# Attention's PSUM banks: two pairs for scores, one for row maxima, joins head by head through the shared bank

## The reference

```python
scores = jnp.einsum('bhid,bhjd->bhij', q, k) * scale     # 2048 x 2048 for each head
scores = jnp.where(causal_mask, scores, min)             # first layer only
attn = jax.nn.softmax(scores, axis=-1)
out = jnp.einsum('bhij,bhjd->bhid', attn, v)
out = out.transpose(0, 2, 1, 3).reshape(b, n, HEADS * HEAD_DIM) @ w_out
```

## Time and profile before

| | us |
|---|---|
| runs shown: median (lowest, highest) | 5976.87 (5966.03, 5989.33) |
| the profiled execution | 5959.15 |
| its span | 5957.9 |
| first attention, steps | from 110 to 1195 |
| second attention, steps | from 2320 to 2957 |
| third attention, steps | from 3280 to 4150 |
| fourth attention, steps | from 4436 to 5889 |

### The profile page before, as it was taken

How to read it: one execution, slowest core, us unless ns; L and a number is a source line. 1 busy time by engine, 2 the same in 40 slices (tenths; PEclk the granted TensorE clock), 3 DMA queues, 4 the chain that set the end, 5 groups by cost and what they waited for, 6 DMA issues and landing times. The chain is left out here.

```text
span 5957.9 us, 69438 instructions
## 1 busy us (share of the span) xinstructions
PE 4932.2 (83%) x27568; PEld 2398.2 (40%) x27568; DVE 3519.1 (59%) x5322; ACT 2358.2 (40%) x3274; POOL 1865.1 (31%) x900
## 2 busy tenths in 40 slices
PE   6888898957767776777767999998679999999996
PEld 3444444445445553333333222222344444444443
DVE  4667666554444545777733777784446666666664
ACT  2333332333333333444422666665134443444433
POOL 0444353610111102655710000000015555555554
PEclk8989898977878876888988999999789999999998
DMA  0000000000000000000000000000000000000000
GB/s 28 3 3 4 3 3 3 1 17 9 5 16 5 5 5 3 2 1 2 1 20 2 1 2 1 2 1 2 7 5 1 3 3 3 3 1 3 3 1 14
DMA packets 53011, 28.19 MB, mean 5 GB/s; under 512 B 30116, under 2 KB 48976, under 8 KB 52432
## 3 DMA queue, kind: packets, MB, share of 16 engines
q1 hardware_dynamic: 52688, 23.75, 1.5%
HBM read 22.68 MB, written 1.05 MB: 4 GB/s over the span
## 5 line engine op out<-in xcount | busy, mean ns | idle before, releaser
L784 DVE TENSOR_REDUCE L_part<-banks 128x2 f32<-128x1024 f32 (+2 forms) x1600 | 1885.1, 1188 | 949.9 <-PE banks L634 850.9
L769 ACT ACTIVATE L_weights<-banks 128x1024 f32<-128x1024 f32 (+1 forms) x1600 | 1544.1, 997 | 1529.6 <-PE banks L667 1304.3
L697 PE MATMUL banks<-L_weights,L_V 128*32 128x512 f32 (+3 forms) x6400 | 1511.5, 621 | 6.5 <-ACT L_weights L769 4.5
L977 POOL TENSOR_TENSOR L_wsum<-L_wsum,L_weights 128x1024 f32<-128x1024 f32 (+1 forms) x448 | 972.5, 2171 | 68.4 <-ACT L_weights L769 2.8
L960 POOL TENSOR_TENSOR L_wsum<-L_wsum,L_two 128x1024 f32<-128x1024 f32 x240 | 569.2, 2372 | 1241.9 <-DVE L_two L950 1240.6
L697 PEld LDWEIGHTS banks<-L_weights,L_V 128*64 128x64 f32 (+1 forms) x6400 | 300.3, 126 | 533.0 <-issue 490.6
L634 PE MATMUL banks<-L_KH,L_QH 64*128 64x512 f32 (+3 forms) x1664 | 380.3, 463 | 59.2 <-DVE L_part L784 42.7
L667 PE MATMUL banks<-L_QH,L_KH 64*128 64x512 f32 (+3 forms) x1664 | 381.9, 455 | 0.0
L950 DVE TENSOR_TENSOR L_two<-L_weights 128x1024 f32<-128x1024 f32 x240 | 327.3, 1364 | 33.5 <-ACT L_weights L769 33.1
L667 PE MATMUL banks<-L_QH,L_KL 64*128 64x512 f32 (+3 forms) x1664 | 332.7, 395 | 0.0
L667 PE MATMUL banks<-L_QL,L_KH 64*128 64x512 f32 (+3 forms) x1664 | 332.6, 395 | 0.0
(11 more groups left out here) (452 smaller groups left out, 6162.6 us busy)
## 6 DMA issues: line engine op xcount, KB each, us to landing
F_tab<-xpos SPq DMA_DIRECT2D x8, 512.0 KB, 3.4
F_h<-L_ffn_h_w SPq DMA_DIRECT2D x2, 1024.0 KB, 7.1
F_wqkv<-L_ffn_wqkv SPq DMA_DIRECT2D x2, 768.0 KB
L_cos<-rope_cos SPq DMA_DIRECT2D x1, 1024.0 KB, 5.1
L_sin<-rope_sin SPq DMA_DIRECT2D x1, 1024.0 KB, 7.2
out<-X SPq DMA_DIRECT2D x1, 1024.0 KB, 5.1
F_w<-L_ffn_w_w SPq DMA_DIRECT2D x3, 256.0 KB, 3.8
F_w<-L_ffn_w SPq DMA_DIRECT2D x2, 341.0 KB
```

Of the source, the lines that this page charges most:

```text
L697: mm = pe.e.matmul(O[r, c:BANK], self.V[g % 2][:, kt, h, :], self.W[x % self.NW][:, y, c:BANK], start=kt < starts, stop=kt >= tiles - starts)
L769: act.e.activation(self.W[x % self.NW][:, :, c:BANK], self.banks(it)[:, :, c:BANK], ACT.Exp, scale=self.scale).then_inc(self.exped, 1)
L784: dve.e.tensor_reduce(self.part[n % 3][:, pr, j, p, :], self.banks(it)[:, :, 0:wide], AX.X, ALU.max).then_inc(self.mx_read, 1)
L977: pool.e.tensor_tensor(acc[:, :, c:BANK], acc[:, :, c:BANK], W[:, :, c:BANK], ALU.add).then_inc(self.summed, 1)
```

## The change

`number` gives scores the pairs 0 and 1 in turn (by the step's parity) and all pieces pair 2. A score now waits for the exponential of the score two steps before; a piece waits for the reduction of the piece before it. This holds in all four attentions.

Where more than two things stand in `ps`, they are put in three places in place of two: ahead of the values of x, between the two values, and behind. With one or two the places are as before.

The join is two items, one for a head, two steps apart. Each goes through bank 7, with four products of 64 rows in place of eight, and four additions on DVE in place of eight. The third attention has its own join and keeps it.

The row of maxima is added by two products of 64 rows within each score (the last term) in place of four of 32 rows for two scores. `negmax` has each maximum on one row, so DVE makes two small reductions for a chunk in the wide attentions in place of four.

The diff, cut to its core:

```diff
-    FREED = {"straight": "dve", "v": "act", "den": "dve", "shift": "act"}
+    FREED = {"straight": "dve", "v": "act", "den": "dve", "shift": "act", "join": "merge"}
...
-        return [(6, ("den", n)), (8, ("join", n))]
+        soon = sum(c[2] for c in self.chunk[n + 1:n + 3]) < 12
+        return [(6, ("den", n)), (6 if soon else 8, ("join", n, 0)), (8 if soon else 10, ("join", n, 1))]
...
+                between = half if len(ps) < 3 else len(ps) - len(ps) // 3
+                half = half if len(ps) < 3 else -(-len(ps) // 3)
...
-                items += [("values", x + 1)] + mid + eager(ys[-1:]) + ps[half:]
+                items += ps[half:between] + [("values", x + 1)] + mid + eager(ys[-1:]) + ps[between:]
...
-            if kind in ("score", "piece") or kind == "join" and kind not in self.FREED:
-                self.pair[it] = len(round) % 3
-                self.held[it] = round[-3] if len(round) > 2 else None
-                round.append(it)
+            if kind in ("score", "piece"):
+                self.pair[it] = 2 if kind == "piece" else it[1] % 2
+                self.held[it] = slots.get(self.pair[it])
+                slots[self.pair[it]] = it
...
-        n = it[1]
-        Y = self.grab(pe, it)
+        n, h = it[1:]
+        Y = self.take(pe, it)
         pe.wait_ge(self.raw_made, n + 1)
+        r = slice(64 * h, 64 * h + 64)
         for j in range(4):
-            for h in range(2):
-                r = slice(64 * h, 64 * h + 64)
-                mm = pe.e.matmul(Y[:, h, j * P:(j + 1) * P], self.raw[n % 2][r, j * P:(j + 1) * P], self.Wo[self.chunk[n][0] % 2][r, :], start=True, stop=True)
-        mm.then_inc(self.joined, 1)
+            mm = pe.e.matmul(Y[:, j * P:(j + 1) * P], self.raw[n % 2][r, j * P:(j + 1) * P], self.Wo[self.chunk[n][0] % 2][r, :], start=True, stop=True)
+        mm.then_inc(self.y_made, 1)
...
-        a = self.columns(n)
-        return [(a, [(q[self.rows(h), :], k[self.rows(h), :]) for h in range(2)]) for q, k in ((self.QH, KH), (self.QL, KH), (self.QH, KL))]
-
-    def shifted(self, pe, it):
-        x = it[1]
-        if x % 2 == 0:
-            both = [self.banks(it), self.grab(pe, ("score", x + 1))]
-            m = self.half(x)[0] % 2 * BANK
-            for h in range(2):
-                for y in range(2):
-                    r, c = slice(64 * h + 32 * y, 64 * h + 32 * y + 32), self.half(x + y)[3]
-                    pe.e.matmul(both[y][:, h, c:BANK], self.onesrow[r, :], self.QM[r, m + c:m + BANK], start=True, stop=False)
-        return True
+        a, m = self.columns(n), n % 2 * BANK
+        return [(at, [(q[self.rows(h), :], k[self.rows(h), :]) for h in range(2)]) for at, q, k in (
+            (a, self.QH, KH), (a, self.QL, KH), (a, self.QH, KL), (m, self.QM, self.onesrow))]
```

More of the change, by code:

```diff
@@ L443, in number @@
         self.qplace, self.qlast, self.pair, self.held = {}, {}, {}, {}
-        freed, parts = {"act": 0, "dve": 0}, {"straight": 0, "low": 0}
-        user, stages, round = {}, [], []
+        freed, parts = {"act": 0, "dve": 0, "merge": 0}, {"straight": 0, "low": 0}
+        user, stages, slots = {}, [], {}
         mx = joins = 0
@@ L544, in grab @@
                 pe.wait_ge(self.exped, held[1] + 1)
-            elif held[0] == "piece":
+            else:
                 pe.wait_ge(self.mx_read, self.mx[held] + 1)
-            else:
-                pe.wait_ge(self.merged, 8 * self.no[held])
         return self.banks(it)
@@ L666, in score @@
             for y, (q, k) in enumerate(term):
-                mm = pe.e.matmul(S[:, y, c:BANK], k[:, kk] if k.shape[1] == T else k[:, :], q[:, a + c:a + BANK], start=t == 0 and not shifted, stop=t == len(terms) - 1 and not (on or cut))
+                mm = pe.e.matmul(S[:, y, c:BANK], k[:, kk] if k.shape[1] == T else k[:, :], q[:, a + c:a + BANK], start=t == 0, stop=t == len(terms) - 1 and not (on or cut))
         for y in range(2):
@@ L809, in most @@
             src = self.part[n % 3][:, h // 2, :, 0:w, h % 2]
-            for r in (self.row[h], self.row[h] + self.again) if self.again else (self.row[h],):
-                last = dve.e.tensor_reduce(self.negmax[n % 2][:, :, r:r + 1], src, AX.X, ALU.max, negate=True)
+            r = self.row[h]
+            last = dve.e.tensor_reduce(self.negmax[n % 2][:, :, r:r + 1], src, AX.X, ALU.max, negate=True)
         last.then_inc(self.maxed, 1)
@@ L817, in merge @@
     def merge(self, dve, it):
-        n = it[1]
-        done = 8 * (self.no[it] - 1)
-        Y = self.banks(it)
-        dve.wait_ge(self.joined, self.no[it])
+        n, h = it[1:]
+        Y = self.ybanked(it)
+        dve.wait_ge(self.y_made, self.y[it] + 1)
         dve.wait_ge(self.inverted, n + 1)
-        dve.wait_ge(self.merged, done)
-        for h in range(2):
-            if h:
-                dve.wait_ge(self.merged, done + 4)
-            for j in range(4):
-                acc = self.core.SACC[:, 4 * self.chunk[n][1] + j, :]
-                dve.e.scalar_tensor_tensor(acc, Y[:, h, j * P:(j + 1) * P], self.rec[n % 2][:, h, j:j + 1], acc, ALU.mult, ALU.add).then_inc(self.merged, 1)
+        dve.wait_ge(self.merged, 4 * (self.no[it] - 1))
+        for j in range(4):
+            acc = self.core.SACC[:, 4 * self.chunk[n][1] + j, :]
+            dve.e.scalar_tensor_tensor(acc, Y[:, j * P:(j + 1) * P], self.rec[n % 2][:, h, j:j + 1], acc, ALU.mult, ALU.add).then_inc(self.merged, 1)
     def low_dve(self, dve, it):
@@ L1001, in once_more @@
         dve.wait_ge(one_made, 2)
-        for r in (0, 32, 64, 96):
+        for r in self.row:
             dve.e.tensor_copy(self.onesrow[r:r + 1, :], one[r:r + 1, :])
```

24 lines of the change are left out of this document (10 added, 14 removed).

## The result

| | before | after |
|---|---|---|
| median of the runs, us | 5974.19 | 6214.23 |
| lowest, highest | 5966.03, 5989.33 | 6211.53, 6229.22 |
| profiled execution's span | 5957.9 | 6227.9 |
| mean granted clock | 0.896 | 0.884 |

The changed kernel is slower: the ratio of the times is 1.0404, with an interval from 1.0377 to 1.0431. The forecast was 6205.

A forecast was written before the change was run, and what follows sets the result against it. PE was taken to set the time in the third and fourth attentions, with a piece's 1.83 us round trip decisive. Third +160, second +58, first +55, fourth -28 gave +245: 5959 became 6204, stated as 6205, range 6080 to 6330.

The forecast's parts named there:

- Part 1, third attention: Third attention's steps: one pair makes each piece wait a 1.83 us round trip, +132 us (105 alternating, 27 side by side).
- The term of the side-by-side pieces: Third attention: 19 distances under 1.2 us between pieces grow from 0.40 to 1.83, +27 us.
- The rival: Third attention: holes of 0.3 us per step lower the clock to 0.87, +75 to +110, 6300 in all; chance 0.13.
- sign of busy time: Third attention: PE would be busy about 85%, from 98% before.
- Part 2, prologues: First chunks' side-by-side pieces come 2.12 apart, not 1.14: third +28, second and fourth +13 each, first +3 us.
- Part 3, pieces of the others: Side-by-side pieces outside the third attention wait for the one pair: fourth +21, first +46, second +30 us.
- Part 4, joins: Fourth, first, second: addition waits go (-58, -32, -29), clock -29, -12; half-joins +29, +29, +15; held-up pieces +31, +31, +29.
- Part 5, row of maxima: 64-row products save 0.17 us per two scores directly behind a piece: fourth -35, first -10 us.
- Only the third pays: First and second attentions' new waits fall into PE's existing idle time: 6091 us in all; chance 0.14.
- The row of maxima costing what it adds: One more pair of products per score pair costs 96 us in place of -45: 6345 in all; chance 0.03.
- Faster through an early release: A reduction frees its pair well before its row ends, so parts 1 to 3 vanish: 5920 us; chance 0.05.
- That the third keeps its banks: The third attention's own class hides the new bank rule: 6044 us in all; chance 0.03.

The follow-up runs named there:

- the kernel with pairs in turn: The changed kernel with scores and pieces sharing all three pairs in turn in all four attentions: 5890.41 us, ratio 0.9849 to the kernel before.
- the kernel with joins and places alone: The kernel before with only joins head by head through bank 7 and pieces in three places: 5936.74 us, ratio 0.9941 to the kernel before.
- the 32-row run: The changed kernel with the row of maxima again added by four products of 32 rows for two scores: 6270.25 us, ratio 1.0484 to the kernel before.
- the first experiment: The changed kernel with scores and pieces taking the three pairs in turn again in the third attention alone: 6014.16 us, ratio 1.0060 to the kernel before.

## Why the prediction was right, and where it was not

The sum of +245 stands against +248 in the attentions. The profiles' spans differ by 270; the other 22 lie outside the attentions, and I didn't follow them. The medians differ by 240, as the profile of before was 15 under its median and that of after 15 over it. So 9 us between 6205 and 6214 is closer than the terms deserve, and it is luck: the third attention was forecast 46 too low (+160 against +206, outside its own range of 130 to 190) and the first 41 too high (+55 against +13.5). The second (+58 against +56) and the fourth (-28 and -28) were right. What the prediction had right is the mechanism: the round trip, where it is paid, and that it outweighs the gain of the rest. By the terms:

**Part 1, third attention: the mechanism was right, the size too small.** Forecast +132, measured +174. The round trip (1.83, measured 1.82) and the term of the alternating pieces (105, measured about 110 once the pieces stand apart) hold. The term of the side-by-side pieces failed: 19 x 1.43 = 27 counted the waits alone, and moving 15 of them gave 64. Behind 13 of them came half-clock work, 140 us in all. I had weighed this as a rival, with "holes of 0.3 are short" against it; that was true of the holes of each step, and I hadn't asked what the 1.3 us waits would do. The bound that I gave, wrong if the granted clock fell under 0.95, was passed: it was 0.93. The rival came true in its mechanism and for half of its price (42 over the forecast, where it had 75 to 110). The Trainium skill's TensorE: Matmul & The Clock Gate, A second HAM failure mode, describes short idle times between groups of matmuls, in a kernel that cycles through PSUM banks, that let the clock swing; what these runs show is narrower, since holes of 0.2 to 0.4 us in each step left the clock alone.

**Its sign of busy time was wrong.** I expected PE busy 85%, and it is 97%. Waits of pieces of over 100 us were right only if weight loads are counted, since most of the standing still is recorded there. In PEld's and PE's own lists of the third attention:

```profile
PEld banks L637 <- DVE L_part L781: 117.2, 374, 2.0
```
```profile
PE banks L637 <- DVE L_part L781: 26.9, 30, 1.4
```

Distances from start to start showed it at once; busy shares did not.

**Part 2, prologues: right.** +28, +13, +13, +3 forecast; 32, 16, 17 and 4 measured. Pieces side by side come 2.12 apart there, as forecast.

**Part 3, pieces of the others.** In the fourth +21 against 14: a piece between two steps of values takes 1.44 in the kernel with pairs in turn, not 1.25, so each of the 37 waits 0.38 and not 0.58, and 37 x 0.38 is the 14. In the second +30 against 9: that stage already waited for reductions, and a good part of the new waits fell into the old ones. In the first +46 against 65, for which half-clock time (84 us more under one pair) is the likely cause, again a price that I hadn't put on a wait.

**Part 4, joins.** No score waits for an addition any more, in any attention, and the fourth has no half-clock stretch behind one. Steps without the one pair and the row of maxima: fourth, forecast -58 - 29 + 29 + 31 = -27, measured -41; first, -32 - 12 + 29 + 31 = +16, measured -28; second, +15, measured 20 to 24. PE around a half-join of the fourth attention in the kernel after (the join is L705, a piece L637, scores L669):

```profile
5270.22 0.82 PE L705 MATMUL banks<-L_Wo,L_raw 64*128 64x128 f32 x5
5270.77 0.50 PE L637 MATMUL banks<-L_KH,L_QH 64*128 64x512 f32 x1
5270.88 0.49 PE L705 MATMUL banks<-L_Wo,L_raw 64*128 64x128 f32 x3
5271.11 0.39 PE L669 MATMUL banks<-L_QH,L_KH 64*128 64x512 f32 x1
5271.13 0.47 PE L637 MATMUL banks<-L_KH,L_QH 64*128 64x512 f32 x1
...
5273.07 0.39 PE L669 MATMUL banks<-L_QM,L_onesrow 64*128 64x512 f32 x1
5273.72 0.50 PE L637 MATMUL banks<-L_KH,L_QH 64*128 64x512 f32 x2 [0.26 <-DVE L_part L781]
```

and DVE beside it, the additions and the reduction behind them:

```profile
5271.41 1.13 DVE L823 SCALAR_TENSOR_TENSOR SACC<-banks,L_rec,SACC 128x128 f32<-128x128 f32 x4 [1.72 <-PE banks L705]
5272.45 1.22 DVE L781 TENSOR_REDUCE L_part<-banks 128x2 f32<-128x1024 f32 x1
```

The half-join lasts 0.91 on its half of the array, as forecast. The piece's product on the other half starts after 0.55, while the join's last three are still running, and its scores run ahead too. That gains nothing in the end: the join's own half starts its last product of the two scores at 5273.07, later by the whole 0.91, and the values behind need both halves.

The next piece starts at 5273.72, 3.50 after the half-join, where I had 3.65 (the reduction follows the additions after 1.04, not 1.15). PE alone would be there after 0.91 + 2.19 = 3.10, so it is held up for 0.4, near my 0.5; the trace records 0.26 of it as idle. The distance is 3.50 or 3.51 behind 60 of the fourth's 64 half-joins, and it is the same behind 60 of 64 where the pairs go in turn. From the kernel with joins and places alone (L713 the half-join, L640 a piece, L789 its reduction):

```profile
5371.71 0.93 PE L713 MATMUL banks<-L_Wo,L_raw 64*128 64x128 f32 x6
...
5375.21 0.50 PE L640 MATMUL banks<-L_KH,L_QH 64*128 64x512 f32 x2
```
```profile
5373.94 1.22 DVE L789 TENSOR_REDUCE L_part<-banks 128x2 f32<-128x1024 f32 x1
```

The piece starts 0.05 after the reduction there too. The order of items explains it: in "two scores, piece, values, piece", the item three before a piece behind two scores is the piece ahead of them, so pairs in turn give it that piece's pair, as one pair for all pieces does. That is one reason why one pair costs the fourth so little.

With that the fourth's terms close. With 32 rows PE would be at the piece after 0.91 + 2.37 = 3.28 and waits 0.23, 60 times, 14 us: -58 - 29 + 29 + 14 = -44 against -41. In the first only 7 of 64 half-joins have the next piece 3.5 behind them, so most of its +31 isn't paid, and its clock gave more: I had 12 us for half-clock time that goes with the waits for additions, and 79 us of such time went (180 to 101), worth up to 40. How much of its -28 is clock isn't tried by itself. The waits of pieces in the whole fourth attention of the changed kernel, and of the one with pairs in turn:

```profile
PE banks L637 <- DVE L_part L781: 46.8, 141, 0.5
```
```profile
PE banks L639 <- DVE L_part L783: 35.8, 105, 0.5
```

So 35.8 of the 46.8 us are not the one pair's. With 32 rows and pairs in turn it is 11.0, as in the kernel before: 25 us of waits came in with the faster row of maxima.

**Part 5, row of maxima.** -35 and -10 forecast, -18 to -20 and -28 to -34 measured in the fourth and first. The sum, 45, was near (46 to 53), the split was wrong. In the fourth the price of 0.17 was right (0.18), the count was not: of the 207 places that I counted some 102 are left where no piece waits. Behind the 60 half-joins, and at 37 places where the pieces stay 2.77 apart, PE comes earlier and waits longer, which is where most of the 25 us of waits come from. In the first I counted only the 60 scores that stand right behind a piece, and some of the gain is clock.

**The fourth attention's -28** is no accident of large errors: joins and row of maxima together -62 forecast and -59 measured, pieces 21 and 14, prologue 13 and 16. Only the share of each part was off, by the waits that the joins bring and the row of maxima runs into.

**The other rivals.** Only the third pays (6091) is wrong in its reason: one pair cost the first attention 69 us and the second 25; the first as a whole grew by only 13.5 because joins and row of maxima gave 56 back, and the second grew by 56. The row of maxima costing what it adds fell with the 32-row run. Faster through an early release fell with the round trip of 1.82. That the third keeps its banks fell with the first experiment.

## What to carry to other kernels

Before giving a producer one buffer, work out its round trip, from its start to the moment when it may write again (here 0.54 + 1.22 + 0.06), and hold it against the distances from start to start that the trace shows now; where the round trip is above the distance and the producer sets the stage's time, the difference is paid each time, whatever the busy shares say. Look too at which item is three before it today: in the fourth attention a piece behind two scores was bound to the piece ahead of them all along. A wait of over one us on PE in a stage that is otherwise full may cost more than itself, by what then runs at half clock, so count long waits apart from short ones, and look whether moving one item by half a step removes them. A change with several parts should be taken apart even when its sum is as forecast: here one line cost 324 us (by the medians) and hid a gain of 84.

## What the hardware showed that was not expected

- Two 64-row halves of the array run on past each other: a product on one half started 0.36 us before its twin (5270.77 and 5271.13), while the other half still worked off a join. The half-join still cost its full 0.91, since the values behind need both halves.
- In an otherwise full stage the granted clock went to half right behind waits of 1.32 us, for 6.8 to 20.5 us with PE busy all along, 13 times in the third attention, and behind three waits of the same length it did not; holes of 0.2 to 0.4 us in each round trip of 1.82 left it at full.
- Four products of 32 rows, which run side by side, among products of 64 rows were dearer than four of 64 rows, which run two by two: 2.37 against 2.19 us across two scores, 53 us for 416 pairs of scores.
